# The down-projection follows two groups behind the up-projection instead of three

## The reference

```
q = layer_norm(x, ln1) @ wq + bq            # 8 x 1024 x 512
k, v = context @ wk + bk, context @ wv + bv # 8 x 64 x 512
s = q k^T / sqrt(32), masked where key index > query index
x1 = x + softmax(s) v @ wo + bo
h = layer_norm(x1, ln2)
out = x1 + gelu(h @ w1 + b1) @ w2 + b2      # w1: 512 x 2048, w2: 2048 x 512
```

## Time and profile before

| | us |
|---|---|
| median of three executions | 1870.21 |
| lowest, highest | 1867.63, 1870.35 |
| the profiled execution, whole | 1869.04 |
| its span | 1867.2 |
| TensorE busy | 1797.5 |
| VectorE busy | 1247.4 |
| ScalarE busy | 636.7 |
| GpSimd busy | 443.0 |

### The profile page before, as it was taken

How to read it: one execution, slowest core, us unless ns; L and a number is a source line. 1 busy time by engine, 2 the same in 40 slices (tenths; PEclk the granted TensorE clock), 3 DMA queues, 4 the chain that set the end, 5 groups by cost and what they waited for, 6 DMA issues and landing times.

```text
span 1867.2 us, 26524 instructions
## 1 busy us (share of the span) xinstructions
PE 1797.5 (96%) x10210; PEld 820.2 (44%) x10210; DVE 1247.4 (67%) x1921; ACT 636.7 (34%) x794; POOL 443.0 (24%) x376
## 2 busy tenths in 40 slices
PE   5559899999999999999999999999999999999999
PEld 3224344444444444444444444444444444444444
DVE  6668768667675767757686676757677576866622
ACT  4635424242332424223242423324242232424211
POOL 3512114131320314122141313203141221413200
PEclk9769999999999999999999999999999999999999
DMA  8230232303123230312323131232303133230200
GB/s 287 57 96 18 46 90 46 91 17 77 45 57 79 46 91 16 79 42 57 80 46 91 15 79 44 57 80 46 91 17 79 41 57 79 46 91 18 51 23 23
DMA packets 287738, 116.27 MB, mean 62 GB/s; under 512 B 262616, under 2 KB 264192, under 8 KB 287616
## 3 DMA queue, kind: packets, MB, share of 16 engines
q1 hardware_dynamic: 287616, 114.61, 27.2%
HBM read 31.22 MB, written 16.78 MB: 26 GB/s over the span
## 4 chain that ended last, share of the span: by engine, by line
PE 90%; DVE 6%; DMA 1%; ACT 1%; issue 1%; SPq 1%; POOL 0%; DVEq 0%; ACTq 0%
PE ff_ps L1081 35%; PE ff_ps L1304 34%; PE at_ps L1081 17%; PE at_ps L1216 2%; PE at_ps L1236 1%; DVE w_all L785 1%; DMA arena<-qT 1%; DVE ssum L1024 0%; DMA arena<-in_L_xattn_wv 0%; DVE arena L785 0%; DVE arena L1008 0%; DVE qT L785 0%; ACT arena L608 0%; DVE smax L1006 0%; DVE xhat L774 0%
## 5 line engine op out<-in xcount | busy, mean ns | idle before, releaser
L1081 PE MATMUL ff_ps<-arena,w_all 128*128 128x512 f16 x3072 | 702.9, 381 | 5.3 <-ACT arena L709 4.3
L1304 PE MATMUL ff_ps<-w_all,arena 128*128 128x512 f16 x3072 | 698.0, 379 | 0.7 <-DVE arena L785 0.7
L1081 PEld LDWEIGHTS ff_ps<-arena,w_all 128*128 128x128 f16 x3072 | 300.5, 98 | 375.5 <-issue 15.3
L1304 PEld LDWEIGHTS ff_ps<-w_all,arena 128*128 128x128 f16 x3072 | 294.4, 98 | 358.4 <-issue 6.4
L709 ACT ACTIVATE arena<-ff_ps,b1p,scales 128x512 f32<-128x512 f32 x256 | 198.6, 776 | 627.4 <-PE ff_ps L1081 627.0
L1054 DVE TENSOR_SCALAR arena<-arena,scales 128x512 f16<-128x512 f32 x256 | 150.1, 586 | 214.8 <-ACT arena L709 212.9
L785 DVE SCALAR_TENSOR_TENSOR arena<-arena,scales 128x512 f16<-128x512 f32 x256 | 239.2, 934 | 9.1
L489 POOL TENSOR_TENSOR rstd<-ve,minus_half 128x1 f32<-128x1 f32 x128 | 86.3, 674 | 561.4 <-DVE ve L757 561.4
L538 POOL TENSOR_TENSOR x_sb<-x_sb,bo_row 128x512 f32<-128x512 f32 x64 | 94.6, 1509 | 349.0 <-PE at_ps L1216 349.0
L648 ACT ACTIVATE norm_hl<-xhat 128x512 f16<-128x512 f32 x120 | 73.9, 628 | 292.7 <-DVE xhat L774 292.7
L543 POOL TENSOR_TENSOR arena<-arena,rsum 128x1024 f32<-128x1024 f32 x64 | 124.8, 1970 | 175.1 <-DVE rsum L1027 175.1
(11 more groups left out here) (144 smaller groups left out, 1359.8 us busy)
## 6 DMA issues: line engine op xcount, KB each, us to landing
x_sb<-in_x SPq DMA_DIRECT2D x64, 256.0 KB, 2.7
out_x<-arena SPq DMA_DIRECT2D x64, 256.0 KB, 2.2
w_all<-in_L_xattn_w SPq DMA_DIRECT2D x6, 1024.0 KB, 10.9
arena<-in_L_xattn_w SPq DMA_DIRECT2D x2, 1024.0 KB, 16.1
v_sb<-v_sb SPq DMA_DIRECT2D x6, 192.0 KB, 3.3
arena<-in_ctx SPq DMA_DIRECT2D x1, 1024.0 KB, 5.6
arena<-in_L_xattn_wk SPq DMA_DIRECT2D x1, 1024.0 KB, 7.7
arena<-in_L_xattn_wv SPq DMA_DIRECT2D x1, 1024.0 KB, 7.7
```

Source lines behind the costliest of these rows:

```text
L1081: last = nc.tensor.matmul(out_ap, s, m, start=(i == 0), stop=(i == n - 1))
L1304: last = nc.tensor.matmul(ff2_ps[:, t, :], pair[:, s, rows], m[:, j], start=(j == 0 and i == 0), stop=(j == NJ - 1 and i == 2))
```

## The change

One constant. It moves every D one group earlier relative to the U's and to the attention steps, and shortens the slot's loop by one group, for every engine.

```
-LAG = 3
+LAG = 2
 GROUPS = NJ + LAG
```

## The result

The changed kernel takes 1872.33 us (median of 20 runs, 1870.30 to 1874.12) against 1868.92 for the kernel before (20 runs, 1867.49 to 1870.63). The ratio is 1.0018, with a 95% interval of 1.0012 to 1.0024: +2.2 to +4.5 us, where +2.8 was forecast. The medians differ by 3.4 us. That is under the 3.7 us that the prediction held to be no telling from none, but with 20 runs of each the interval leaves zero out. The profiled execution took 1871.34 us, its span is 1869.5.

A forecast was written before the change was run, and what follows sets the result against it. TensorE bounds the kernel, busy 1797.5 of 1867.2 us. Terms 0.3 (odd slots) + 2.6 (slot 1 end) - 1.8 (middle's clock) + 1.7 (D15's clock) = +2.8, giving 1873.0 us on the median 1870.21; 8 in 10: 1868.6 to 1876.4.

The forecast's parts named there:

- up to V0, from U0 of slot 1: Slot 1: one more D ahead of Q moves its chain 2.6 us later, and V0 starts another 0.3 late.
- V0 to D15: Slot 1: V0 to V2 runs at the full clock, so the old half-clock loss of 2.1 us goes.
- D15 to the next U0: End of slot 1: half clock behind the new gap ahead of D15 costs +1.7 us.
- Slot end, odd slots: D15 in odd slots 3 to 13 has 0.02 us of slack; hand-over costs 0.04 to 0.05 each, 0.3 in all.
- Slot 1, end: D15 waits 3.48 us for its pair instead of 0.89; the pair comes 2.59 later, so +2.6 us.
- Slot 1, middle: Old 5.47 us gap before V0 splits into 4.2 before D8, waiting for a conversion, and 1.4 before V0; 0 us.
- The clock: Slot 1: D8 gap's 1.7 us loss mostly hidden in V0's wait, old 2.1 saved: net -1.8; D15 gap +1.7.
- The gap ahead of D15: Slot 1 end: gap of 3.3 us as drawn, followed by half clock costing 1.7; nothing if it counts as short.
- Every slot waits: Rival: hand-over at D15 costs 0.27 us in each of slots 2 to 14; 1876.2 us; chance 0.08.
- VectorE absorbs the shift: Rival: in slot 1 VectorE's row, not Q, sets V0, which starts as before; 1870.1 to 1868.4 us; chance 0.12.
- The clock paid twice: Rival: slot 1's half clock behind D8 reaches V0, or V0's gap brings it back; 1874.8 to 1876.8 us; chance 0.15.
- if slot 1 is 130 us or more, the clock term was wrong: Sign in the new profile: slot 1 was forecast at 127 to 128.7 us, in place of 126.2.

The follow-up runs named there:

- e1: The changed kernel run once more with no edit, for a second trace; 1872.95 us, ratio 1.0017 to the kernel before.
- e2: Against the kernel before: D's two groups behind in slot 1 alone, three in all other slots; 1872.14 us, ratio 1.0015.
- e3: Against the kernel before: D's two groups behind in slots 2 to 16, three in slot 1; 1870.39 us, ratio 1.0001.
- e4: Changed kernel with steps A and C of the next chunk's first layer norm moved to position 31, behind pair 15 (the late norm); 1867.92 us.
- e6: Changed kernel with the third quarter of w2 converted ahead of the last quarter of w1; 1871.64 us, ratio 1.0012 to the kernel before.
- e7: As e4, but in slot 1 three groups behind up to group 10, D8 and D9 in group 11 ahead of V0, then two; 1864.23 us.
- e5: Kernel before (three groups behind) with steps A and C of the next chunk's first layer norm at position 31; 1868.13 us, ratio 0.9995.
- e8: Kernel before with D's one group behind (LAG = 1); 1978.8 us, ratio 1.0587, 2 runs.

## Why the prediction was right, point by point

The forecast, +2.8 us, lies inside the measured interval, and its places and releasers are what the runs show. Its clock terms were less sure than it says, and that they add up has some luck in it. The table compares traces in pairs. e1 and the kernel before have nearly the same gelu's gap near the start of slot 1 (4.56 and 4.31 us), and so have e2 and e3 (5.30 and 5.31), which differ in slot 1 in just the change; the first trace after (5.20) has no such match with the kernel before.

| step | predicted | e1 against before | e2 against e3 | first trace after against before |
|---|---|---|---|---|
| up to V0, from U0 of slot 1 | +2.6 +0.3 | 85.44 - 82.67 = +2.8 | 87.09 - 83.36 = +3.7 | 87.22 - 82.67 = +4.6 |
| V0 to D15 | -2.1 | 38.99 - 40.93 = -1.9 | 39.20 - 41.76 = -2.6 | 39.11 - 40.93 = -1.8 |
| D15 to the next U0 | +1.7 | 4.13 - 2.60 = +1.5 | 4.16 - 2.60 = +1.6 | 4.23 - 2.60 = +1.6 |
| six odd slots | +0.3 | +0.3 | +0.3 (from e3) | +0.2 |
| sum | +2.8 | +2.7 | +3.0 | +4.6 |

- **Slot end, odd slots.** Right: 0.03 to 0.05 us each; shown by e2 and e3.
- **Slot 1, end.** Right in size: 0.67 + 2.77 = 3.4 us of drawn waits against the forecast 3.3. It was called D15's wait alone; D14 waits a part of it for pair 14, which was not looked up. e4 shows that it is pair 15's place behind A and C.
- **Slot 1, middle.** The 4.2 us gap before D8 was 4.11, with the named releaser, and V0 runs at the full clock. e6 confirms that the conversion sets D8, and that the chain behind Q sets how early V0 can start; in the changed kernel itself V0 starts a little later than that, behind D9. A 0.1 us wait of D4 for a conversion, not named, changes nothing.
- **The clock.** The step that is loose. The loss behind the D8 gap was taken as 1.7 from one row of slot 0; it is 10.30 - 3 x 2.59 = 2.5 us in the first trace and also in e2 and e4, and 9.55 - 7.77 = 1.8 only in e1. The old order's loss behind the V0 gap, taken as 2.1, is 2.5 in e3 (V0 to V2 in 5.94 us). In e2 against e3 the two errors, 0.8 and 0.4 us, work against each other, and that is luck: nothing in the prediction says so. And a term was left out: the gelu's gap before U2 lies ahead of all that moved, as the prediction says, but the half clock behind it differs between executions of one kernel (slot 1 of the old order: 126.20 and 127.71 us). That is why one pair of traces reads +4.4 for slot 1 and another +2.4. With slot 0 it makes the spread of each kernel's times, some 3 us. The sign that the prediction gave, "if slot 1 is 130 us or more, the clock term was wrong", was set against the one trace of 126.2; the first trace (130.6) and e2 (130.45) meet it, but 130.45 is only 2.7 above e3.
- **The gap ahead of D15** of 2.77 us cost 1.5 to 1.6, as forecast, and not nothing; behind D14's 0.67 us no loss is seen. The Trainium skill ("TensorE: Matmul & The Clock Gate", "Why this matters for your kernels") warns of a fall to half rate behind longer gaps than these; here the clock fell behind 2.77 us and behind e7's 2.24 us too, so the measurements decide.
- **The rivals.** Every slot waits: refuted by e2 and e3. VectorE absorbs the shift: refuted. The start of V0 does not show it, since V0 stands behind D9 in the changed kernel, but SyncE's issue of V0's transposing DMAs does. Here it is in the kernel before, e1, e3 and the first trace after:

```profile
193.15 17.29 SPq L428 DMA_TRANSPOSE arena<-qT  x4
...
194.34 17.32 SPq L428 DMA_TRANSPOSE arena<-qT  x4
...
194.16 17.34 SPq L428 DMA_TRANSPOSE arena<-qT  x4
...
194.19 17.35 SPq L428 DMA_TRANSPOSE arena<-qT  x4
```

It ends 80.32 us behind slot 1's U0 in the kernel before and 82.69 in e1, 81.05 in e3 and 83.74 in the first trace after: 2.4 and 2.7 us later, about the whole D of 2.59. The clock paid twice: V0's half clock did not come back, V0 to V2 is 3.46 or 3.47 us in all five traces with two groups throughout slot 1 (the first trace, e1, e2, e4, e6). The other half of this rival came near. It was to decide where V0 starts more than 1.8 us after 215.4; counted from U0, the first trace has it 1.9 us after 215.4, and its sum of +4.6 is the rival's lower end; e1 has it 0.2 after. A part of the 1.9 lies in the gelu's half clock and not behind D8.

What stays open: why the half clock behind the same gap is longer in one execution than in another, and what makes slot 0 differ by up to 3 us between executions.

## What to carry to other kernels

When an in-order engine is full, moving work earlier on it can only spend slack: take, for each consumer, the time at which its operand was ready and the start that it would have, one by one over all blocks and all slots, the odd first ones above all. A gap that is set by a chain is filled by putting work behind the chain's first step and ahead of the gap; the same work put ahead of the first step moves the chain, and what it fills of the gap comes back as lateness (changed kernel +3.4 us; e7 -5.0, of which the late norm has some 1.1).
Look in VectorE's order for work that nobody waits for soon and that stands ahead of a result that TensorE wants next; moving it back took 5.0 us off the changed kernel (e4 against e1), more than the 3.4 us that the shorter distance between producer and consumer had cost, and made that distance matter no more. In the kernel before it gained nothing that is clear of the noise (e5).

## What was not expected of the hardware

The same gap of 4.11 us before D8 was followed by different losses, 2.5 and 1.8 us, in two executions of one kernel. The gelu's gap itself was 4.2 to 5.3 us long over the ten traces other than e8's, while U2 behind it began 12.2 us after U0 in all of them: U0 and U1 ahead of it ran at different clocks. A gap of 2.24 us ahead of V0 was followed by the half clock at U12, one of 1.68 us (e6) was not. In every odd slot from 3 to 13 of e8 there are gaps of 2.15 and 2.46 us, and they were followed by it in some slots and not in others: slot 5 took 113.8 us and slot 7 115.5 with the same waits.
